# Row maxima of the scores: one VectorE instruction for each tile, four PSUM banks in turn

## The reference, cut to what matters

```python
qkv = hidden_states @ W_qkv                                  # (4, 2048, 768)
scores = jnp.einsum('bhqd,bhkd->bhqk', q, k)                 # 64 matrices of 2048 x 2048
scores = scores + compute_bias(rel_emb, S, S)
attn = jax.nn.softmax(scores.astype(jnp.float32), axis=-1).astype(scores.dtype)
out = jnp.einsum('bhqk,bhkd->bhqd', attn, v)
```

## Time and profile before

| | |
|---|---|
| median of 3 runs | 3145.61 us (3145.13 to 3150.0) |
| profiled execution, its own time | 3145.94 us |
| its span, first to last instruction | 3143.8 us |
| TensorE busy | 3116.9 us (99%) |
| VectorE busy | 2816.8 us (90%) |
| ScalarE busy | 2438.4 us (78%) |
| GpSimd busy | 1299.5 us (41%) |
| mean granted TensorE clock | 0.997 |

### The profile page before, as it was taken

How to read it: one execution, slowest core, us unless ns; L and a number is a source line. 1 busy time by engine, 2 the same in 40 slices (tenths; PEclk the granted TensorE clock), 3 DMA queues, 4 the chain that set the end, 5 groups by cost and what they waited for, 6 DMA issues and landing times.

```text
span 3143.8 us, 72337 instructions
## 1 busy us (share of the span) xinstructions
PE 3116.9 (99%) x28162; PEld 1773.6 (56%) x28162; DVE 2816.8 (90%) x3745; ACT 2438.4 (78%) x4665; POOL 1299.5 (41%) x1920
## 2 busy tenths in 40 slices
PE   8999999999999999999999999999999999999998
PEld 7888888454545444454454544445444444445447
DVE  5577765999999999999999999999999999999933
ACT  4443454788888888888888888888888888888884
POOL 1112113444444444444444445444444444444445
PEclk9999999999999999999999999999999999999999
DMA  4633334332222222222222222222222221222105
GB/s 137 155 113 99 98 105 99 54 68 38 38 38 38 38 38 38 38 38 38 38 38 38 38 38 38 38 38 38 38 37 38 38 38 38 38 38 38 24 10 193
DMA packets 135588, 174.37 MB, mean 55 GB/s; under 512 B 52960, under 2 KB 99680, under 8 KB 128912
## 3 DMA queue, kind: packets, MB, share of 16 engines
q1 hardware_dynamic: 135248, 169.75, 25.9%
HBM read 109.26 MB, written 56.69 MB: 53 GB/s over the span
## 4 chain that ended last, share of the span: by engine, by line
PE 80%; DVE 1%; POOL 0%; DMA 0%; ACT 0%; issue 0%; SPq 0%; POOLq 0%; ACTq 0%
PE ps L1171 38%; PE ps L1188 25%; PE ps L1193 9%; PE ps L1160 7%; PE ps L1227 1%; DVE max_half L1110 1%; DMA total_sb<-o_sb 0%; POOL prob L1074 0%; ACT prob L1027 0%; POOL k_st L260 0%; SPq L932 0%; POOL vr L1058 0%; DVE wo_parts L1144 0%; ACT o_sb L1014 0%; POOL vx L1085 0%
## 5 line engine op out<-in xcount | busy, mean ns | idle before, releaser
L1110 DVE TENSOR_REDUCE max_half<-ps 128x1 f32<-128x512 f32 (+1 forms) x2666 | 2407.8, 945 | 36.1 <-PE ps L1160 27.2
L1027 ACT ACTIVATE prob<-ps 128x512 f32<-128x512 f32 x4096 | 2157.0, 600 | 356.7 <-PE ps L1171 353.1
L1074 POOL TENSOR_TENSOR prob<-prob,near 128x224 f32<-128x224 f32 (+2 forms) x1664 | 976.0, 601 | 1376.6 <-ACT prob L1027 1369.9
L1160 PE MATMUL ps<-k_st,q_st 48*128 48x512 f32 x3968 | 1484.8, 461 | 0.4 <-DVE max_half L1110 0.3
L1171 PE MATMUL ps<-q_st,k_st 49*128 49x512 f32 x4096 | 1345.5, 430 | 3.2 <-PEq L267 2.3
L1171 PEld LDWEIGHTS ps<-q_st,k_st 49*128 49x128 f32 x4096 | 660.7, 184 | 862.8 <-ACT prob L1027 723.9
L1188 PE MATMUL ps<-prob,vr 128*32 128x384 f32 x4864 | 757.0, 498 | 0.0
L1160 PEld LDWEIGHTS ps<-k_st,q_st 48*128 48x128 f32 x3968 | 639.8, 184 | 62.5 <-DVE max_half L1110 10.3
L1188 PE MATMUL ps<-prob,vx 128*32 128x384 f32 x3328 | 594.5, 500 | 2.4 <-POOL prob L1074 1.3
L1193 PE MATMUL ps<-prob,vx 128*32 128x128 f32 x7040 | 276.0, 277 | 0.5 <-POOL prob L1074 0.4
L730 PE MATMUL ps<-xnt,w_parts 128*128 128x512 f32 x1152 | 267.0, 392 | 3.4 <-DVE xnt L521 2.0
(11 more groups left out here) (72 smaller groups left out, 1145.2 us busy)
## 6 DMA issues: line engine op xcount, KB each, us to landing
qk_parts<-parts SPq DMA_DIRECT2D x64, 512.0 KB, 4.7
q_st<-qk_parts SPq DMA_DIRECT2D x192, 128.0 KB, 3.8
k_st<-qk_parts SPq DMA_DIRECT2D x192, 128.0 KB, 5.5
near<-bias_near SPq DMA_DIRECT2D x64, 352.0 KB, 6.2
x_sb<-in_L_attn_hidden_states SPq DMA_DIRECT2D x16, 512.0 KB, 7.3
base_rows<-x_sb SPq DMA_DIRECT2D x16, 512.0 KB, 5.6
recip_rows<-recip_all SPq DMA_DIRECT2D x256, 32.0 KB, 1.8
bias_near<-bias_line SPq DMA_DIRECT2D x8, 704.0 KB
```

The costliest lines, as they stand in the source:

```text
L1027: nc.scalar.activation(prob[:, t % PROBS, CH * j:CH * (j + 1)], ps[:, bank_of(at)], ACT.Exp).then_inc(drained, 1)
L1074: nc.gpsimd.tensor_tensor(at, at, near[n % GROUP][:, side, c0:c0 + q1 - q0], ALU.mult).then_inc(near_done, 1)
L1110: nc.vector.tensor_reduce(max_half[:, m % 2].rearrange("p i c -> p (i c)")[:, k:k + len(banks)], tiles, AX.X, ALU.max) \
L1160: mm = nc.tensor.matmul(ps[:, MAX_BANK + bank], query_block(q_st[u][0:ROWS], k // CPB), k_st[u][0:ROWS, CH * (k % CPB):CH * (k % CPB + 1)] ...
```

## The change

`max_groups` makes one group of each tile. The banks are used in turn, tile `k` of a head has bank `k % 4`, and a bank is written again when the group four before is done. Every maxima matmul now signals `max_ready`, and VectorE runs 64 instructions for a head instead of 43. Matmuls, their order on TensorE, and everything else stay as they are; `max_count`, `combine` and the waits take their numbers from `MAX_ORDER` as before.

```diff
@@ -133,29 +133,14 @@
 NEAR_UP_TO = [sum(len(visit_parts(visit)) for visit in VISITS[:v]) for v in range(NV + 1)]
 
 
-SINGLE = CPB - 1
-SHARED = 1
-
-
 def max_groups():
 
-    freed = {bank: bank - CPB for bank in range(CPB)}
-    groups, order, pairs = [], {}, 0
+    groups, order = [], {}
     for m in range(LEAD, NH):
-        k = 0
-        for v, visit in enumerate(VISITS):
-            for size in ([1, 2] if len(visit) == WIDE else [1] * len(visit)):
-                at = len(groups)
-                first = SHARED - pairs % 2
-                banks = range(first, first + 2) if size == 2 else range(SINGLE, SINGLE + 1)
-                pairs += size == 2
-                tiles = sorted(range(size), key=lambda i: banks[i] == SHARED)
-                for j, i in enumerate(tiles):
-                    order[m, k + j] = at, k + i, banks[i], freed[banks[i]], j == size - 1
-                for bank in banks:
-                    freed[bank] = at
-                groups.append((m, k, banks))
-                k += size
+        for k in range(CPB * KB):
+            at, bank = len(groups), k % CPB
+            order[m, k] = at, k, bank, at - CPB, True
+            groups.append((m, k, range(bank, bank + 1)))
     return groups, order
```

## The result

The changed kernel takes 3087.03 us, the median of 4 runs from 3086.41 to 3087.64. The kernel before, run beside it, takes 3145.37 (3144.59 to 3150.0). The ratio is 0.9813, with an interval of 0.9801 to 0.9826: 58 us less.

A forecast was written before the change was run, and what follows sets the result against it. A 1.83 us loop through the pairs' shared bank was taken as the bound. VectorE's 38.27 + 0.11 + 0.09 + 0.13 + 0.14 = 38.74 a head against 39.70 saves 58.5 over 61 heads: 3145.9 to 3087 us, range 3066 to 3126.

The forecast's parts named there:

- The loop through the shared bank: Between TensorE and VectorE before: matmul to pair start 0.55, pair 1.22, release 0.06, together 1.83, taken as the visit's period.
- A single in a chain: On VectorE: each one-tile reduction behind another takes a slot of 0.598, so 64 take 38.27 us a head.
- Rival 1: On VectorE: each reduction keeps the 0.608 slot of a start from rest, giving 3126 us; chance 0.10.
- rival 2: On VectorE: chained singles are cheaper, 0.58 each, saving 128 us at the edge, 3060 with TensorE's exposed loads; chance 0.05.
- the small slots: VectorE's small work a head: reciprocals +0.11, transpose +0.09, combine's wait +0.13 and its own slot 0.14.
- A stock of half a microsecond: Between TensorE and VectorE: a tile is ready after 2.49, VectorE gets there after 2.99; the 0.50 gap keeps it fed.
- rival 3: On TensorE: a second maxima matmul a visit waits too, making the visit 1.88 and the kernel 3224 us; chance 0.05.
- rival 4: On VectorE: singles don't overlap, 64 x 0.69 + 0.6 = 44.8 a head, 3460 us; chance 0.03.
- Head 0: nothing: In head 0, where the clock is still low, no gain was expected; the saving was summed over 61 heads.
- The mean of 681 ns: Sign in the profile after: the reduction of maxima, 3968 times, has a mean duration near 681 ns.
- rivals 1 or 5: Rival 5: another loop holds the visit at 1.82, giving 3146 us, chance 0.05; a 691 ns mean would speak for either.
- TensorE's own limit: On TensorE without the wait: a visit takes 1.68, or 1.78 if the weight load stays exposed; a head 36.8 us.

## Why the prediction was right, point by point

The forecast was 3087, a head of 38.74 us; measured 3087.03 and 38.74. The agreement of a head is earned by the terms below, which came out to a few hundredths each. That of the whole to 0.03 us is partly luck: the runs of one kernel lie 1.2 us apart, and between the two profiled executions head 0 gave 2.06 us that the sum didn't have and the first block took 1.35.

- *The loop through the shared bank bounded the kernel before.* Right in kind: shorter pairs bring twice what shorter lone tiles do, and one-tile reductions on the old banks are slower than before. Incomplete: from matmul to pair start takes 0.53, not the 0.55 of the sum, so that this round alone gives 1.80. The 1.82 belongs to a round over two visits that has the single's slot in it, and shortening the single brought 24 us. The change removed both rounds, so the forecast didn't depend on it.
- *A single in a chain holds VectorE 0.598.* Right: 27 slots in 16.10 us. The chain of another operation from PSUM was the right row to take. Rival 1 (0.608) and rival 2 (0.58) are out, and the small slots (0.13 from combine to reduction, 0.12 from transpose to reduction, 0.15 from reciprocals to reduction) are as summed.
- *A stock of half a microsecond keeps VectorE fed.* Right inside a head, where no idle time is left: in the steady visits the first tile's reduction starts 1.02 to 1.03 behind its matmul (medians over the heads), 0.46 more than the 0.56 or 0.57 of a reduction that starts at once; 0.50 had been worked out. At the head's start it was not a stock but a near tie: the combine ran while the first tile was being made, and the kernel with the later combine finds VectorE waiting. The forecast there (the stock covers it) gave the right time for a reason only half right.
- *No two waits in a visit* (rival 3), *overlap between singles* (rival 4): right. The second maxima matmul has 0.39 and the third score follows the second by 0.24. The overlap is even larger than assumed, 0.09 on the mean (0.691 less 0.598). The Trainium skill, "VectorE: DVE Perf Modes", section "The DRAIN you can't avoid", says that the next instruction doesn't start until the pipe is empty. By that each slot would have been 0.69; the runs show 0.598. The same section adds that a next instruction which isn't held starts earlier, and the prediction left this out. The slots agree with it as far as they go: what would hold an instruction no run here shows.
- *Head 0: nothing.* Wrong by 2.1 us, given back in part by a first block that ended 1.35 later. About half of the 2.1 goes with head 0's granted clock, 0.85 before and 0.88 after; the other half is about what every head gained, and the sum had left head 0 out. Why the first block ended later stays open.
- *The mean of 681 ns* was wrong: it is 691, and by the text it should have spoken for rivals 1 or 5. The starts decided, not the durations.
- TensorE's own limit was put at 1.68 to 1.78 a visit and 36.8 a head. The 36.70 us a head with short reductions and short exponentials, with visits of 1.68, confirm the lower end. Missed was the limit between, the three score banks at 37.70: ScalarE was called no limit by its busy time of 34.1 a head, which leaves out how long a bank is held. It would have capped the gain at 122 us, so the edge of rival 2 (128) couldn't have been reached.

## What to carry to other kernels

Where two engines hand a few buffers round, compute for each buffer the time from its filling to its release and on to its next filling, and compare that with the engines' work: a buffer held by a longer instruction can cost more than the instruction saves. An engine that is busy 99% is at its limit only if its starts lie a slot apart; compare start to start, not duration. And test a limit by shortening the suspected work by a little: what comes back as time, and where it stops coming, gives the order of the limits.

## What the runs showed of the hardware

The duration that the profile gives a reduction isn't what it costs. In the changed kernel's chain the starts stay 0.598 apart while the durations grow (least, median and greatest of 3968):

```profile
L1095 DVE TENSOR_REDUCE max_half<-ps x3968: 637/694/706, 547.1 to 2951.9; 128x1 f32<-128x512 f32 x199
```

So neighbours overlap by about 0.10 where they overlapped by 0.08 in the trace of before. Why the row of an instruction grows in a long chain, these runs don't show. The slot follows the columns closely: 0.598 for 512, 0.580 for 496. A pair in a chain holds the engine for 1.13 (3.49 less 1.22, halved, in the kernel with pairs only), so that two tiles in one instruction save VectorE 0.07 and hold both banks for the whole 1.22.
